# Attention on one Trainium2 core: the product with V in two halves of its columns, the maximum pieces of a step in three parts around them

## The chip, the core and the metric

The kernel runs on one core of a Trainium2 chip. The metric is the device time of one execution in microseconds. Work is spread over the engines of the core: TensorE (PE in the rows, its weight loads PEld), VectorE (DVE), ScalarE (ACT), GpSimd (POOL) and the DMA queues, issued here by SyncE (SP). Each engine runs its own instruction stream in order, and they meet at semaphores.

## The reference, cut to what matters

The program is half a feed-forward block, a two-way Mamba block, and the feed-forward block again. Each feed-forward block begins with causal attention over 4 sequences of 2048 tokens, with 16 heads of 16 that share 4 key and value heads:

```
attn = jnp.einsum('bqhd,bkhd->bhqk', q, k) * scale
attn = jnp.where(causal, attn, jnp.float32(-jnp.inf))
attn = jax.nn.softmax(attn, axis=-1)
out = jnp.einsum('bhqk,bkhd->bqhd', attn, v).reshape(B, S, C)
```

The change is in this attention alone, which is run twice in an execution.

## The kernel before

`attention` makes N = 16 iterations, one for each sequence and key head; an iteration serves the 4 query heads (REP) of that key head. In an iteration there are NB = 40 steps. A step is one block (qb, kb): 512 query tokens (qb of 0 to 3) against 128 key tokens (kb up to the diagonal). On the diagonal only the last 384, 256 or 128 query columns of a block are computed.

For each step s the engines do this:

- TensorE, `score` (L739): the transposed scores of the 4 heads, keys on partitions and queries along the row, one PSUM bank for each head (banks 0 to 3). Two heads lie in different row halves of the array and run beside each other. Heads 0 and 1 wait until ScalarE has read the banks of heads 0 and 1 of the step before, heads 2 and 3 until it has read those of 2 and 3.
- ScalarE (L794): two exponentials of two heads each, PSUM to SBUF tile `e`, with room for 4 steps.
- GpSimd (L641): the causal mask on diagonal blocks of `e`.
- TensorE, `weighted` (L705), for the step LAG = 2 earlier: the product of `e` with V in f32, accumulated in bank 4 over a qb. Each head takes 32 columns of the array, so the four heads run beside each other. In the trace each f32 matmul of the program is two records, so that one product is eight.
- TensorE, `maximum` (L674, and L678 for a diagonal mask): the softmax needs the row maximum of the scores before the exponential, so scores with queries on partitions are computed a second time, ahead of use, in 144 pieces an iteration. A piece is up to 512 columns in one PSUM bank. Pieces come in pairs: even ones lie in the lower row half of the array, odd ones in the upper, and two of a pair run beside each other.
- VectorE, `reduce` (L833): one maximum over each piece.

The pieces, the turned outputs and the turned maxima go round three PSUM banks (5, 6, 7) in the order of use. TensorE waits in `bank_is_free` until the use three places earlier has been read.

`share(s)` says which pieces a step has; `spread` has dealt them out by a cost for each step. Steps 5, 7, 16 and 27 have six pieces, step 2 has none, steps 3, 6, 10, 11, 14, 22, 23, 26, 38 and 39 have two, and the other 25 have four. The last iteration of a call has only the pieces of its steps 0 to 7. In steps 2, 6, 14 and 26 an output is copied to tile `o` by ScalarE (L809) and turned on TensorE (L713); VectorE then normalises it (L851, L854). In steps 8 and 19 the maxima are turned (L692).

The order on TensorE inside a step is written out by hand. Before, it is: four scores, the first part of the pieces (two of four, two of six, none of two), the whole product with V, the rest of the pieces, and then what is turned.

Of the kernel before, what the change touches and what calls it, by code (L numbers as in the profile page):

```python
# [14 lines left out]
CH = 512  # L15
# [15 lines left out]
class Phase:  # L31
# [9 lines left out]
    def sb(self, name, shape, dtype=F32):  # L41
        return self.ctx.enter_context(self.nc.sbuf_tensor(f"{self.tag}_{name}", shape, dtype))

    def sem(self, name):
        self.sems.append(self.nc.alloc_semaphore(f"{self.tag}_{name}"))
        return self.sems[-1]
# [364 lines left out]
VW = 32  # L411
# [3 lines left out]
def attention(nc, tag, psum, ident, unscale, qp, kp, v_in, ao, B, S):  # L415
# [6 lines left out]
    N = B * KVH  # L422
    NBUF = 3
    assert N > 1 and (N - 1) % NBUF == 0
    blocks = [(qb, kb) for qb in range(NQB) for kb in range(TT * (qb + 1))]
    NB = len(blocks)
# [10 lines left out]
    PB = 4  # L437
    LAG = 2
    E0, PV0 = 1, PB - 1

    def diag(s):
        qb, kb = blocks[s]
        return kb - TT * qb

    def closes(s):
        return s >= 0 and blocks[s][1] == TT * (blocks[s][0] + 1) - 1
# [52 lines left out]
    def share(s, last=False):  # L499

        return [("tail", n) for n in tail[s]] if s < D else [] if last else [("head", n) for n in head[s - D]]
# [14 lines left out]
    def out_of(it, qb):  # L516

        return it - 1 if qb == NQB - 1 else it
# [10 lines left out]
    with Phase(nc, tag) as ph:  # L529
# [3 lines left out]
        V = [sb(f"v{p}", [P, S // P, VW]) for p in range(NBUF)]  # L533
        E = sb("e", [P, PB, REP, CH])
# [12 lines left out]
        s_ps, e_ready, masked, pv = sem("s_ps"), sem("e_ready"), sem("masked"), sem("pv")  # L547
        o_sb, oT_ps, recip, normed, stored = sem("o_sb"), sem("oT_ps"), sem("recip"), sem("normed"), sem("stored")
        BANK_O = 4
# [14 lines left out]
        with nc.Block() as block:  # L564
# [81 lines left out]
            def _(pe):  # L646
# [3 lines left out]
                def bank_is_free(when, it, use):  # L650

                    found = used_before(when, it, use)
                    if found is None:
                        pe.wait_ge(m_red, T)
                        return
                    at, (kind, n) = found
                    if kind == "tail":
                        pe.wait_ge(m_red, at * NP + n + 1)
                    elif kind == "head":
                        pe.wait_ge(m_red, (at + 1) * NP + n + 1)  # L660
                    elif kind == "out":
                        pe.wait_ge(normed, out_of(at, n) * NQB + n + 1)
                    elif kind == "max":
                        pe.wait_ge(m_high, 2 * (at + 1 - n) + n + 1)
                        pe.wait_ge(m_low, 2 * (at + 1 - n) + n + 1)
# [16 lines left out]
                def maxima(when, it, par, todo):  # L682

                    for kind, n in todo:
                        if (kind, n) == ("head", 0):
                            pe.wait_ge(loaded[(par + 1) % NBUF], LOADS * ((it + 1) // NBUF + 1))
                        bank_is_free(when, it, (kind, n))
                        maximum(par if kind == "tail" else (par + 1) % NBUF, n, turn_bank(when, (kind, n)))
# [2 lines left out]
                    hold(pe, n_max, 2 * it + g + 1, pe_passed)  # L691
                    nc.tensor.transpose(psum[0:MR, turn, 0:P], nm[:, :, :].rearrange("p h i -> p (h i)"), ident[:, :]).then_inc(mT_ps, 1)  # L692

                def weighted(it, par, s):

                    qb, kb = blocks[s]
                    off = max(diag(s), 0) * P
                    pe.wait_ge(e_ready, E0 + 2 * (it * NB + s + 1))
                    if diag(s) >= 0:
                        n_diag = sum(diag(z) >= 0 for z in range(s + 1))  # L700
                        pe.wait_ge(masked, it * NQB * TT + n_diag)
                    if kb == 0:
                        pe.wait_ge(o_sb, it * NQB + qb)
                    for h in range(REP):
                        ins = nc.tensor.matmul(psum[32 * h:32 * h + VW, BANK_O, off:CH], V[par][:, kb, :],  # L705
                                               E[:, s % PB, h, off:CH], start=kb == 0, stop=closes(s),
                                               tile_position=(0, 32 * h))
                    ins.then_inc(pv, 1)

                def turn_output(it, qb, turn):  # L710
                    pe.wait_ge(o_sb, it * NQB + qb + 1)
# [12 lines left out]
                def step(it, par, when):  # L724
                    q, k = Q[par], K[par]
                    last = (par + 2) % NBUF
                    for s in range(NB):
                        qb, kb = blocks[s]
                        off = max(diag(s), 0) * P
                        if s == 0:  # L730
                            pe.wait_ge(m_in, PUTS * (2 * it + 1))
                        if s == s_half:
                            pe.wait_ge(m_in, PUTS * (2 * it + 2))

                        def score(h):
                            if h % 2 == 0:
                                pe.wait_ge(e_ready, E0 + 2 * (it * NB + s) + h // 2 - 1)
                            at = slice(h % 2 * ROWS, h % 2 * ROWS + SROWS)
                            ins = nc.tensor.matmul(psum[:, h, off:CH], k[at, kb * P:(kb + 1) * P],  # L739
                                                   q[at, qb * CH // (HALF * P), h // 2, qb * CH % (HALF * P) + off:qb * CH % (HALF * P) + CH],  # L740
                                                   start=True, stop=True, tile_position=(h % 2 * ROWS, 0))
                            if h % 2:
                                ins.then_inc(s_ps, 1)

                        todo = share(s, when == "last")
                        half = len(todo) // 4 * 2
                        score(0)
                        score(1)  # L750
                        score(2)
                        score(3)
                        maxima(when, it, par, todo[:half])
                        if s >= LAG:
                            weighted(it, par, s - LAG)
                        elif when != "first":
                            weighted(it - 1, last, NB + s - LAG)
                        maxima(when, it, par, todo[half:])
                        out = back_close(s)
                        if out is not None and not (when == "first" and s <= LAG):  # L760
                            bank_is_free(when, it, ("out", out))
                            turn_output(out_of(it, out), out, turn_bank(when, ("out", out)))
                        if s == TURN1:
                            bank_is_free(when, it, ("max", 1))
                            turn_maxima(it, 1, turn_bank(when, ("max", 1)))
                        if s == TURN0 and when != "last":
                            bank_is_free(when, it, ("max", 0))
                            turn_maxima(it + 1, 0, turn_bank(when, ("max", 0)))
                phase_steps(pe, step)
                for s in range(NB - LAG, NB):  # L770
                    weighted(N - 1, (N - 1) % NBUF, s)
                pe.wait_ge(m_red, N * NP)
                pe.wait_ge(m_low, 2 * N)
                pe.wait_ge(normed, N * NQB - 1)
# [1368 lines left out]
```

## Time and profile before

| What | Value |
|---|---|
| Median of 3 runs | 8606.55 us (8600.69 to 8619.03) |
| The profiled execution: its own time | 8600.78 us |
| The profiled execution: its span | 8599.0 us |
| First attention's iterations, start of scores of the first to that of the last | 272.5 to 1770.1 us |
| Second attention's | 6528.5 to 8033.9 us |
| TensorE busy in the span | 7649.1 us (89%) |
| VectorE busy | 7351.8 us (85%) |
| ScalarE busy | 5097.1 us (59%) |

An engine's busy time counts the spans of its instructions laid over one another. The matmuls are pipelined, and each record reaches some 0.2 us beyond the issue of the next, so that the time a matmul takes of TensorE is read here from the start of one group to the start of the next, not from its duration.

### The profile page before, as it was taken

How to read it: one execution, taken by the hardware profiler on the slowest of the kernel's cores; microseconds unless marked ns; L12 is line 12 of the kernel's file. 1: busy time of each engine (PE TensorE's matmuls, PEld its weight loads, DVE VectorE, ACT ScalarE, POOL GpSimd, SP SyncE). 2: the span in 40 equal slices, each digit the busy share in tenths (PEclk: the TensorE clock that was granted, in tenths of full speed). 3: DMA queues.
4: the chain of work that ended last, by engine and by line, in shares of the span. 5: the costliest groups of instructions: out<-in, count | busy, mean ns of one | idle time of the engine just before them, and what ended most of it. 6: DMA issues, size and time to landing. Idle time of an engine off the chain costs nothing. (4 is left out here: it accounts for less than half of the span.)

```text
span 8599.0 us, 133275 instructions
## 1 busy us (share of the span) xinstructions
PE 7649.1 (89%) x38899; PEld 3079.3 (36%) x38900; DVE 7351.8 (85%) x10758; ACT 5097.1 (59%) x7698; POOL 3712.1 (43%) x1828
## 2 busy tenths in 40 slices
PE   6999999989898888888888888888779999999899
PEld 3333333335543333333333333333443333333355
DVE  6988888958868999999979999999458988988588
ACT  3577777762256666666656555555224777777622
POOL 0010111000018999999969999999300010011000
PEclk8899999989999999999999999999987999999899
DMA  6101111012262222222233333333561011011122
GB/s 174 17 20 19 19 21 25 13 45 75 67 234 85 83 82 83 83 83 82 82 100 101 101 99 101 101 97 100 166 196 29 20 19 20 19 19 19 37 72 65
DMA packets 542812, 617.68 MB, mean 72 GB/s; under 512 B 195969, under 2 KB 353921, under 8 KB 538081
## 3 DMA queue, kind: packets, MB, share of 16 engines
q1 hardware_dynamic: 537568, 576.35, 22.8%
q0 software_dynamic: 4608, 33.56, 1.9%
q8 instruction: 314, 5.14, 0.2%
q14 instruction: 322, 2.63, 0.1%
HBM read 411.41 MB, written 163.76 MB: 67 GB/s over the span
## 5 line engine op out<-in xcount | busy, mean ns | idle before, releaser
L833 DVE TENSOR_REDUCE ffn_att_mx<-psum 128x1 f32<-128x512 f32 (+3 forms) x4608 | 2725.7, 653 | 354.9 <-PE psum L674 199.4
L794 ACT ACTIVATE ffn_att_e<-psum,unscale 128x1024 f32<-128x1024 f32 (+3 forms) x2560 | 2378.7, 985 | 750.0 <-PE psum L739 744.0
L641 POOL TENSOR_SCALAR_AFFINE_SELECT ffn_att_e<-ffn_att_e 128x512 f32<-128x512 f32 x512 | 326.1, 637 | 3007.8 <-ACT ffn_att_e L794 3007.8
L674 PE MATMUL psum<-ffn_att_k,ffn_att_q 48*128 48x512 f16 (+3 forms) x5120 | 1433.5, 366 | 173.5 <-DMA ffn_att_v<-v 58.1
L1697 POOL TENSOR_TENSOR scan_r_h<-scan_r_h,scan_r_cs 128x1024 f32<-128x1024 f32 x512 | 1207.7, 2451 | 148.2 <-ACT scan_r_state L1860 144.7
L1697 POOL TENSOR_TENSOR scan_f_h<-scan_f_h,scan_f_cs 128x1024 f32<-128x1024 f32 x512 | 1204.7, 2446 | 117.0 <-ACT scan_f_state L1860 114.8
L705 PE MATMUL psum<-ffn_att_e,ffn_att_v 128*32 128x512 f32 (+3 forms) x10240 | 1234.2, 555 | 8.0 <-ACT ffn_att_o L809 2.6
L1776 PE MATMUL psum<-scan_f_h,ident 128*128 128x512 f32 x2048 | 1002.5, 630 | 83.9 <-POOL scan_f_h L1697 83.4
L1776 PE MATMUL psum<-scan_r_h,ident 128*128 128x512 f32 x2048 | 980.6, 620 | 75.3 <-POOL scan_r_h L1697 74.5
L1900 ACT ACTIVATE psum<-scan_r_dt,scan_r_an 128x512 f32<-128x512 f32 x1024 | 698.0, 682 | 460.2 <-DVE scan_r_h L1992 460.0
L674 PEld LDWEIGHTS psum<-ffn_att_k,ffn_att_q 48*128 48x128 f16 x5120 | 394.5, 94 | 1554.0 <-DVE ffn_att_mx L833 1268.3
L1900 ACT ACTIVATE psum<-scan_f_dt,scan_f_an 128x512 f32<-128x512 f32 x1024 | 697.5, 681 | 422.6 <-DVE scan_f_h L1992 422.3
L739 PE MATMUL psum<-ffn_att_q,ffn_att_k 50*128 50x512 f16 (+3 forms) x5120 | 809.0, 353 | 62.4 <-issue 27.3
L1992 DVE TENSOR_TENSOR_SCAN scan_r_h<-psum,scan_r_state,scan_r_db 128x512 f32<-128x512 f32 x704 | 845.2, 1261 | 6.1 <-ACT psum L1900 6.0
L1992 DVE TENSOR_TENSOR_SCAN scan_f_h<-psum,scan_f_state,scan_f_db 128x512 f32<-128x512 f32 x704 | 840.8, 1260 | 8.6 <-ACT psum L1900 8.5
L1776 PEld LDWEIGHTS psum<-scan_f_h,ident 128*128 128x128 f32 x2048 | 389.3, 199 | 678.6 <-issue 437.6
L1776 PEld LDWEIGHTS psum<-scan_r_h,ident 128*128 128x128 f32 x2048 | 386.1, 196 | 647.8 <-issue 438.6
L1180 DVE SCALAR_TENSOR_TENSOR ffn_out_acc<-psum,ffn_out_comb,ffn_out_acc 128x256 f32<-128x256 f32 x896 | 433.3, 484 | 64.9 <-PE psum L1045 29.8
L678 PE MATMUL psum<-ffn_att_mask,ffn_att_pick 64*128 64x128 bf16 x4096 | 435.2, 221 | 0.0
L1958 DVE TENSOR_TENSOR scan_r_db<-scan_r_du,psum 128x2048 f32<-128x2048 f32 x177 | 404.8, 2287 | 24.5 <-DVE scan_r_h L1992 3.9
L1958 DVE TENSOR_TENSOR scan_f_db<-scan_f_du,psum 128x2048 f32<-128x2048 f32 x177 | 404.9, 2287 | 23.7 <-PE psum L1751 3.4
L983 POOL TENSOR_TENSOR ffn_out_ul<-ffn_out_uT,ffn_out_uh 128x1024 f16<-128x1024 f32 x32 | 68.1, 2128 | 811.5 <-ACT ffn_out_uh L1094 811.5
(261 smaller groups left out, 9895.2 us busy)
## 6 DMA issues: line engine op xcount, KB each, us to landing
scan_f_cs<-scan_f_bcd SPq DMA_DIRECT2D x264, 256.0 KB, 3.1
scan_r_cs<-scan_r_bcd SPq DMA_DIRECT2D x264, 256.0 KB, 3.2
scan_f_bs<-scan_f_bcd SPq DMA_DIRECT2D x82, 256.0 KB, 3.4
scan_r_bs<-scan_r_bcd SPq DMA_DIRECT2D x82, 256.0 KB, 3.4
scan_f_win<-xp SPq DMA_DIRECT2D x18, 1036.0 KB, 6.7
scan_r_win<-xp SPq DMA_DIRECT2D x18, 1036.0 KB, 7.0
mamba_out_ys<-yz SPq DMA_DIRECT2D x18, 1024.0 KB, 7.3
scan_r_yi<-y SPq DMA_DIRECT2D x17, 1024.0 KB, 9.3
```

The source lines that it names most:

```text
L674: ins = nc.tensor.matmul(psum[:, turn, j * w:(j + 1) * w], q[at, i // HALF, pair, i % HALF * P:(i % HALF + 1) * P], k[at, c * P:c * P + w] ...
L678: ins = nc.tensor.matmul(psum[:, turn, (j + 1) * w - P:(j + 1) * w], pick[rows_at, 1 - hh + z, :], mask[rows_at, 1 - hh + z, :], start=Fal ...
L705: ins = nc.tensor.matmul(psum[32 * h:32 * h + VW, BANK_O, off:CH], V[par][:, kb, :], E[:, s % PB, h, off:CH], start=kb == 0, stop=closes(s ...
L739: ins = nc.tensor.matmul(psum[:, h, off:CH], k[at, kb * P:(kb + 1) * P], q[at, qb * CH // (HALF * P), h // 2, qb * CH % (HALF * P) + off:q ...
L794: nc.scalar.activation(E[:, s % PB, 2 * hp:2 * hp + 2, off:CH], psum[:, 2 * hp:2 * hp + 2, off:CH], ACT.Exp, scale=unscale[:, 0:1]).then_i ...
L833: nc.vector.reduce_max(mx[:, hh * 2 + pairs[0]:hh * 2 + pairs[1], i // HALF, i % HALF, c // TT], psum[:, turn, 0:(pairs[1] - pairs[0]) * w ...
L1180: nc.vector.scalar_tensor_tensor(acc[:, e % 2, :], psum[:, BANKS_E[(n // 2) % 4], (e % 2) * C:(e % 2 + 1) * C], comb[par][:, t, e:e + 1], ...
L1697: nc.gpsimd.tensor_tensor(hh, hh, cs[:, n % NCS, :].unsqueeze(1).to_broadcast([P, 2, CH]), ALU.mult).then_inc(hc_ready, 1)
L1776: ins = nc.tensor.matmul(psum[:, m, :], ident[:, :], h[n % NH][:, m, :], start=False, stop=n == DS - 1)
L1900: nc.scalar.activation(psum[:, BANK_A + k % 2, :], dt[par][:, m, :], ACT.Exp, scale=an[:, m, n:n + 1]).then_inc(decay, 1)
L1958: nc.vector.tensor_tensor(db[b_turn(par, n)][:, :, :], du[par][:, :, :], psum[:, BANK_B, :].unsqueeze(1).to_broadcast([P, DM, CH]), ALU.mu ...
L1992: nc.vector.tensor_tensor_scan(h[n % NH][:, m, flip], psum[:, BANK_A + k % 2, flip], made_b[:, m, flip], state[:, n, m:m + 1], ALU.mult, A ...
```

## The change

The product with V is issued in two halves of its columns (`part` 0 and 1, the middle being halfway between `off` and 512). The pieces of the step are cut in three: a first third, the first half of the product, a second third, the second half, and the last third. With four pieces the parts are 1, 1, 2, with two pieces 0, 1, 1, and with six 2, 2, 2. The sum of pieces of each step, their order, and all other engines' instructions stay as they were. Semaphore `pv` is raised at the second half alone, as the wait on `e` stands ahead of both halves.

```diff
-                def weighted(it, par, s):
+                def weighted(it, par, s, part):
...
                     off = max(diag(s), 0) * P
+                    mid = (off + CH) // 2
+                    lo, hi = (off, mid) if part == 0 else (mid, CH)
                     pe.wait_ge(e_ready, E0 + 2 * (it * NB + s + 1))
...
                     for h in range(REP):
-                        ins = nc.tensor.matmul(psum[32 * h:32 * h + VW, BANK_O, off:CH], V[par][:, kb, :],
-                                               E[:, s % PB, h, off:CH], start=kb == 0, stop=closes(s),
+                        ins = nc.tensor.matmul(psum[32 * h:32 * h + VW, BANK_O, lo:hi], V[par][:, kb, :],
+                                               E[:, s % PB, h, lo:hi], start=kb == 0 and part == 0, stop=closes(s) and part == 1,
                                                tile_position=(0, 32 * h))
-                    ins.then_inc(pv, 1)
+                    if part == 1:
+                        ins.then_inc(pv, 1)
...
                         todo = share(s, when == "last")
-                        half = len(todo) // 4 * 2
+                        cuts = [len(todo) * k // 3 for k in range(4)]
                         score(0)
                         score(1)
                         score(2)
                         score(3)
-                        maxima(when, it, par, todo[:half])
-                        if s >= LAG:
-                            weighted(it, par, s - LAG)
-                        elif when != "first":
-                            weighted(it - 1, last, NB + s - LAG)
-                        maxima(when, it, par, todo[half:])
+                        for part in range(2):
+                            maxima(when, it, par, todo[cuts[part]:cuts[part + 1]])
+                            if s >= LAG:
+                                weighted(it, par, s - LAG, part)
+                            elif when != "first":
+                                weighted(it - 1, last, NB + s - LAG, part)
+                        maxima(when, it, par, todo[cuts[2]:])
```

On TensorE, in steps 22 and 23 and the start of 24, the program before has these rows. The names are: `ffn_att_q,ffn_att_k` with `ffn_att_k` last are scores of a step, `ffn_att_k,ffn_att_q` a maximum piece, `ffn_att_e,ffn_att_v` the product with V of one head.

```order
L739 MATMUL psum<-ffn_att_q,ffn_att_k 128x256 x4
L705 MATMUL psum<-ffn_att_e,ffn_att_v 32x512 x4
L674 MATMUL psum<-ffn_att_k,ffn_att_q 128x512 x2
L739 MATMUL psum<-ffn_att_q,ffn_att_k 128x128 x4
L705 MATMUL psum<-ffn_att_e,ffn_att_v 32x384 x4
L674 MATMUL psum<-ffn_att_k,ffn_att_q 128x512 x2
L739 MATMUL psum<-ffn_att_q,ffn_att_k 128x512 x4
```

The same two steps of the changed program, on the same engine:

```order
L742 MATMUL psum<-ffn_att_q,ffn_att_k 128x256 x4
L707 MATMUL psum<-ffn_att_e,ffn_att_v 32x256 x4
L674 MATMUL psum<-ffn_att_k,ffn_att_q 128x512
L707 MATMUL psum<-ffn_att_e,ffn_att_v 32x256 x4
L674 MATMUL psum<-ffn_att_k,ffn_att_q 128x512
L742 MATMUL psum<-ffn_att_q,ffn_att_k 128x128 x4
L707 MATMUL psum<-ffn_att_e,ffn_att_v 32x192 x4
L674 MATMUL psum<-ffn_att_k,ffn_att_q 128x512
L707 MATMUL psum<-ffn_att_e,ffn_att_v 32x192 x4
L674 MATMUL psum<-ffn_att_k,ffn_att_q 128x512
L742 MATMUL psum<-ffn_att_q,ffn_att_k 128x512 x4
```

The pair of pieces, which stood together behind the product, is now one piece between its halves and one behind them.

The second place is step 28 with the scores of step 29, where a step has four unmasked pieces of 512 columns; TensorE before:

```order
L739 MATMUL psum<-ffn_att_q,ffn_att_k 128x512 x4
L674 MATMUL psum<-ffn_att_k,ffn_att_q 128x512 x2
L705 MATMUL psum<-ffn_att_e,ffn_att_v 32x512 x4
L674 MATMUL psum<-ffn_att_k,ffn_att_q 128x512 x2
L739 MATMUL psum<-ffn_att_q,ffn_att_k 128x512 x4
```

And in the changed program, at the same place:

```order
L742 MATMUL psum<-ffn_att_q,ffn_att_k 128x512 x4
L674 MATMUL psum<-ffn_att_k,ffn_att_q 128x512
L707 MATMUL psum<-ffn_att_e,ffn_att_v 32x256 x4
L674 MATMUL psum<-ffn_att_k,ffn_att_q 128x512
L707 MATMUL psum<-ffn_att_e,ffn_att_v 32x256 x4
L674 MATMUL psum<-ffn_att_k,ffn_att_q 128x512 x2
L742 MATMUL psum<-ffn_att_q,ffn_att_k 128x512 x4
```

Of the first pair one piece now stands ahead of the product and one between its halves; the second pair stays together behind it.

## Rows read from the trace of the kernel before

**Rows 1.** The page's busy time of each engine, of the whole span.

```profile
PE 7649.1 (89%) x38899; PEld 3079.3 (36%) x38900; DVE 7351.8 (85%) x10758; ACT 5097.1 (59%) x7698; POOL 3712.1 (43%) x1828
```

**Rows 2.** Windows, one iteration each: start:end, length, busy by engine, clock, DMA share, GB/s.

```profile
472.26:571.12 98.86, 94.10 (x789) 32.12 (x786) 88.09 (x157) 76.61 (x86) 10.19 (x16) 0.98 0.11 20
...
1077.71:1175.40 97.69, 92.86 (x789) 31.83 (x787) 88.09 (x157) 76.60 (x86) 10.20 (x16) 1.00 0.10 21
```

**Rows 3.** Windows, steps 10 to 11, 14 to 20, 26 to 37, 38 to 39.

```profile
1103.39:1106.38 2.99, 2.99 (x42) 0.99 (x38) 2.16 (x4) 2.11 (x4) 0.83 (x3) 1.00 0.02 3
...
1110.74:1130.70 19.96, 18.87 (x145) 6.21 (x145) 18.01 (x33) 15.80 (x17) 0.00 (x0) 1.00 0.04 8
...
1140.74:1172.41 31.67, 30.29 (x231) 8.96 (x233) 29.62 (x51) 25.90 (x26) 1.13 (x2) 1.00 0.03 5
1172.41:1175.40 2.99, 2.99 (x38) 1.00 (x34) 2.36 (x4) 2.10 (x4) 0.78 (x2) 1.00 0.00 0
```

**Rows 4.** Waits, iteration at 1077.71 us: total us, times, longest.

```profile
PEld psum L674 <- DVE ffn_att_mx L833: 39.8, 76, 0.8
...
DVE ffn_att_mx L833 <- PE psum L674: 4.7, 8, 1.0
```

**Rows 5.** Timeline of TensorE, two steps of four pieces: start us, us, group.

```profile
454.43 0.90 PE L674 MATMUL psum<-ffn_att_k,ffn_att_q 48*128 48x512 f16 x2
455.25 1.07 PE L705 MATMUL psum<-ffn_att_e,ffn_att_v 128*32 128x512 f32 x8
456.25 0.39 PE L674 MATMUL psum<-ffn_att_k,ffn_att_q 48*128 48x512 f16 x2
456.48 0.60 PE L739 MATMUL psum<-ffn_att_q,ffn_att_k 50*128 50x512 f16 x4
456.91 0.90 PE L674 MATMUL psum<-ffn_att_k,ffn_att_q 48*128 48x512 f16 x2
```

**Rows 6.** Timeline, TensorE alone at 457.45 us: the second piece of the last group.

```profile
457.43 0.39 PE L674 MATMUL psum<-ffn_att_k,ffn_att_q 48*128 48x512 f16 x1
```

**Rows 7.** Timeline of VectorE in the same steps, one reduction a row.

```profile
455.39 0.68 DVE L833 TENSOR_REDUCE ffn_att_mx<-psum 128x1 f32<-128x512 f32 x1
...
455.99 0.68 DVE L833 TENSOR_REDUCE ffn_att_mx<-psum 128x1 f32<-128x512 f32 x1
...
456.68 0.69 DVE L833 TENSOR_REDUCE ffn_att_mx<-psum 128x1 f32<-128x512 f32 x1
```

**Rows 8.** Timeline of ScalarE in the same steps, with the idle time before.

```profile
456.90 2.12 ACT L794 ACTIVATE ffn_att_e<-psum,unscale 128x1024 f32<-128x1024 f32 x2 [0.37 <-PE psum L739]
```

**Rows 9.** Timeline of TensorE in steps 10, 11 and the start of 12, 13.

```profile
1103.39 0.39 PE L739 MATMUL psum<-ffn_att_q,ffn_att_k 50*128 50x256 f16 x4
1103.71 1.06 PE L705 MATMUL psum<-ffn_att_e,ffn_att_v 128*32 128x512 f32 x8
1104.70 0.40 PE L674 MATMUL psum<-ffn_att_k,ffn_att_q 48*128 48x512 f16 x2
1104.93 0.28 PE L678 MATMUL psum<-ffn_att_mask,ffn_att_pick 64*128 64x128 bf16 x4
1105.05 0.28 PE L739 MATMUL psum<-ffn_att_q,ffn_att_k 50*128 50x128 f16 x4
1105.26 0.85 PE L705 MATMUL psum<-ffn_att_e,ffn_att_v 128*32 128x384 f32 x8
1106.04 0.40 PE L674 MATMUL psum<-ffn_att_k,ffn_att_q 48*128 48x512 f16 x2
...
1107.64 0.64 PE L705 MATMUL psum<-ffn_att_e,ffn_att_v 128*32 128x256 f32 x8
1108.22 0.69 PE L674 MATMUL psum<-ffn_att_k,ffn_att_q 48*128 48x512 f16 x2
```

**Rows 10.** Windows, step 6 in two iterations; the clock is the third number from the end.

```profile
485.66:489.77 4.11, 4.11 (x19) 1.25 (x18) 2.59 (x5) 2.12 (x2) 0.00 (x0) 0.58 0.65 145
688.36:690.94 2.58, 2.58 (x20) 0.91 (x21) 2.14 (x4) 2.02 (x2) 0.00 (x0) 1.00 0.98 191
```

More of the change, by code:

```diff
@@ L770, in _ @@
                 for s in range(NB - LAG, NB):
-                    weighted(N - 1, (N - 1) % NBUF, s)
+                    weighted(N - 1, (N - 1) % NBUF, s, 0)
+                    weighted(N - 1, (N - 1) % NBUF, s, 1)
                 pe.wait_ge(m_red, N * NP)
```

## The prediction, made before the changed kernel was run

> **What bounds the kernel now.** The page's busy times [rows 1] say only that TensorE and VectorE are both near full. The change touches the attention, so I cut one iteration out by windows: from the first scores to those of the next iteration it lasts 97.69 us at full clock, 98.86 us where the clock is 0.98 [rows 2]. VectorE is busy for 88.1 of it, TensorE for 92.9, ScalarE for 76.6: no engine is idle enough to be left out, and which one sets the pace must be read from each kind of step.
>
> *Steps of four pieces (25 of 40).* The scores of this step are issued at 456.48 us and the first piece at 456.91 (0.43 for the scores), the pair behind the product at 456.25, 0.23 ahead of them; the product takes 1.00, from 455.25 to 456.25 [rows 5]. The step's period is 2.48 (454.43 to 456.91). The two pieces ahead of the product are not issued together: the second comes at 457.43, 0.52 behind the first [rows 6], as its bank is still being reduced; such waits for VectorE are 39.8 us of an iteration at the weight loads [rows 4] (much of this lies under a running product). On VectorE one reduction starts 0.60 after the other if its piece is there (455.39, 455.99), and once a step 0.69 after it (456.68) [rows 7]. So VectorE needs 4 x 0.60 = 2.40 of 2.48: it is the bound, and the largest gain to be had in such a step is 0.08. ScalarE is busy for 2.12 and idle for 0.37 [rows 8].
>
> *Steps of two pieces (10).* Steps 10 and 11 last 2.99 together and TensorE is busy in all of it, VectorE for 2.16; steps 38 and 39 read alike [rows 3]. There TensorE's own stream is the bound: scores, product, pair, with no wait in it [rows 9].
>
> Where VectorE is idle in an iteration, 4.7 us and more of it are waits for pieces [rows 4], mostly behind these light steps.
>
> **The change part by part.** It adds no work to VectorE, ScalarE, GpSimd or a queue. On TensorE it does three things.
>
> (a) A product in halves. From product to the next group a 512-column product takes 1.00 [rows 5], one of 384 columns 0.78 (1105.26 to 1106.04), one of 256 columns 0.58 (1107.64 to 1108.22) [rows 9]. That is 0.21 for each 128 columns and some 0.14 that does not depend on the columns. Two halves of 256 take 1.14 to 1.16 by the rounding of the starts; I take 1.14: **+0.14**; two of 192 (0.47 each, an estimate on the same line) +0.16.
>
> (b) A switch from a piece into a product. The four scores of 256 columns need 0.22 (half of 0.43), but the product follows 0.32 behind them [rows 9], so entering a product costs 0.10. A lone piece at 512 columns is a stream of 0.21 (its 0.22 as half the scores), and with the switch 0.32.
>
> (c) A broken pair. A pair leaves 0.23 behind it [rows 5]; two lone pieces take 0.21 each. A masked pair takes 0.35 (1104.70 to 1105.05 [rows 9]), so that a mask adds 0.12 for the pair, and adds it twice if the pair is broken.
>
> For a step of two: before 0.10 + 1.00 + 0.23 behind the scores, after 0.10 + 0.57 + 0.32 + 0.57 + 0.23: **+0.46**, and +0.58 if masked. For a step of four, before 0.33 + 1.00 + 0.23 = 1.56, after 0.32 + 0.57 + 0.32 + 0.57 + 0.23 = 2.01: **+0.45**, so that TensorE's stream grows from 1.99 to 2.44 with the scores. For a step of six (pairs stay whole) +0.24; for step 2 some +0.04.
>
> Below nothing these costs cannot go: no matmul is taken away. Their upper end is that a half costs as much as the nearest whole in the rows, 0.58 and not 0.57, and that each lone piece with its mask waits for its bank as well.
>
> Three lots of steps answer differently.
>
> *Light steps bound by TensorE.* All of it shows: steps 10 and 11 +0.58 and +0.57 (masked), 22 and 23 +0.46 and +0.45, 39 +0.45, 3 (384 columns, masked) +0.50, 38 +0.28, since its 1.72 now holds a wait for VectorE that its stream of 1.54 does not need. Step 6 +0.45. Sum **+3.7**. Nothing covers them: ScalarE and VectorE have less to do in these steps than 1.5 us.
>
> *Steps of four at 512 columns.* The period becomes the larger of TensorE's 2.44 and VectorE's 2.40, where it was 2.48. Scores 2 and 3 wait for ScalarE, whose 2.12 for a step begin 0.42 behind the scores (456.48, 456.90) [rows 5, 8], which leaves 2.45. So unmasked steps gain 0.03 to 0.04. Masked ones (18, 30) had 2.71 and get 2.44 + 3 x 0.12 = 2.80, so lose 0.08; steps 15 and 34, with a masked pair broken first, lose 0.05. Steps 14 to 20 now take 19.96 and steps 26 to 37 31.67, with VectorE busy 18.0 and 29.6 [rows 3]. Adding the new streams, with six-piece steps at VectorE's pace, I get about 19.8 and 31.4: **-0.4** together.
>
> *The rest* (0 to 2, 4, 5, 7 to 9, 12, 13, 21, 24, 25) has small products (64 or 128 columns a half) or slack: +0.13 at step 4, some 0.1 at others, together **+0.2**.
>
> An iteration gets +3.5 us. Two calls have 15 iterations each with all pieces (the last has few pieces and stays with ScalarE): 30 x 3.5 = 105 us. Against it stands the clock: step 6 takes 4.11 at a granted clock of 0.58 in one iteration and 2.58 at full clock in another [rows 10]; about half of the iterations have such a drop, behind steps in which TensorE did little. A denser TensorE may lose some: 8 us off. That gives 8600.8 + 97 = 8698 for the profiled kind of run, whose time stands 5.8 below the median of the runs shown; for the median 8606.6 + 97, I say **8700**.
>
> **A rule weighed against the rows.** The row says that a halved product costs 0.14 more. The Trainium skill (TensorE: Matmul & The Clock Gate, Back-to-back issue gap) gives the isolated spacing of matmuls as columns over 2.4 GHz plus 2.5 ns, by which a halving would cost some 5 ns. The same page (Part 3, The mechanism) lets a weight load overlap matmuls in flight only where the row group differs, by which product and piece, which share rows, can't hide each other's load; the trace agrees with the latter, with the 0.10 at the entry and the 0.14 at the exit.
>
> **The rivals.**
>
> 1. *As worked out: TensorE's stream is what the light steps wait for, +3.5 an iteration.* Own range +1.4 to +6.3 an iteration (steps of four gain the whole 0.08 each at one end, at the other they keep half of the waits that the trace now shows over the larger of the streams, some 6 of 98), 8640 to 8790. Chance 0.62.
>
> 2. *The switches are hidden.* If the weights of the next group come in while the last one streams, (a) and the second 0.10 fall away and a step of two pays only for the broken pair, 0.22. For: the program allows loads ahead. Against: the row of 256 columns pays the whole 0.14 where a pair follows. Seven light steps then cost 1.6 and twenty steps of four gain 0.08 each, 1.6: no change, 8606. Chance 0.08.
>
> 3. *Faster: VectorE is kept fed and TensorE's slack absorbs everything.* TensorE's streams alone, summed over the 40 steps by the costs above, go from 75 to 93 us, under 97.7. If the three banks let a TensorE-bound step lend time to its VectorE-bound neighbour, the iteration goes to some 95: 30 x -2.5, 8530. It decides if, behind a light step, the reductions still queued cover the longer stream, so that VectorE is never idle there. For: a piece between the halves arrives 0.5 earlier than before in terms of TensorE work. Against: three banks hold 1.8 us of reductions, and VectorE is idle already in the light steps. Chance 0.15.
>
> 4. *Much slower: two engines at the same pace.* A step of four has 2.44 on TensorE, 2.40 on VectorE and 2.45 through ScalarE. Any wait for one now delays the others, where 0.5 of TensorE slack took it up. If the surplus over the larger stream, about 6 us an iteration today, stays as it is on top of a sum of 100, an iteration takes 106: +8.4, 8850. Against: in steady steps every bank comes free 0.1 or more ahead of its use. Chance 0.15.
>
> **How the numbers follow.** The time is that of rival 1. Differences within 0.2% (17 us) can't be told from none. Slower: 0.62 + 0.15, plus a little of 2: 0.78. Faster 0.15, same 0.07. The range goes from 8590, which takes in rival 2, to 8800, which takes in all of 1 and the near end of 4; outside are most of 3 and part of 4, about 0.2.
>
> **What would show it.** In the changed profile: the product's group of 256 columns followed 0.57 later by the piece (right for a); a lone piece followed 0.32 later by the product (b, c); steps 10 to 11 at 4.1 us and 38 to 39 at 3.7, all busy on TensorE; steps of four at 2.44 to 2.46; the waits of L674's weights for VectorE well below 39.8 an iteration. Wrong would be: steps of two that did not grow (rival 2), steps 14 to 20 or 26 to 37 shorter by over 1 us (rival 3), or longer by over 1 (rival 4).

## The result, and the profile after

The changed kernel takes 8711.53 us (median of 4 runs, 8708.62 to 8716.01), the kernel before, beside it, 8605.13 us (4 runs, 8600.69 to 8619.03). The ratio is 1.0122, with an interval of 1.011 to 1.0134: slower by 1.2%. The forecast was 8700 in a range of 8590 to 8800.

The page after, with its span and the busy time of each engine:

```profile
span 8712.4 us, 154363 instructions
...
PE 7853.2 (90%) x49139; PEld 3311.1 (38%) x49140; DVE 7408.8 (85%) x10758; ACT 5091.6 (58%) x7698; POOL 3710.0 (43%) x1828
```

Against [rows 1] TensorE has 10,240 more matmuls and is busy 204 us longer, and the span grew by 113.4 (8712.4 - 8599.0). VectorE has the same instructions.

Windows of the kernel after, columns as in [rows 2]: one whole iteration at full clock, steps 10 to 11, 14 to 20, 26 to 37, and 38 to 39.

```profile
1427.94:1528.20 100.26, 97.55 (x1112) 38.44 (x1108) 89.72 (x157) 76.42 (x86) 10.15 (x17) 1.00 0.10 21
1453.74:1457.54 3.80, 3.80 (x56) 1.49 (x51) 2.77 (x5) 2.10 (x4) 1.18 (x3) 1.00 0.01 2
1462.29:1482.74 20.45, 19.86 (x202) 7.35 (x199) 18.29 (x33) 15.46 (x17) 0.00 (x0) 1.00 0.04 9
1493.24:1524.56 31.32, 31.19 (x328) 10.96 (x329) 29.49 (x51) 25.86 (x26) 0.98 (x2) 1.00 0.03 6
1524.56:1528.20 3.64, 3.64 (x54) 1.32 (x48) 3.15 (x6) 2.10 (x4) 1.13 (x3) 1.00 0.00 0
```

The iteration went from 97.69 [rows 2] to 100.26: +2.57, and TensorE is now busy for all but 2.7 us of it. Against [rows 3] steps 10 to 11 lost 0.81, steps 38 to 39 0.65, steps 14 to 20 0.49, and steps 26 to 37, of which ten have four pieces, gained 0.35.

The waits of the same iteration, columns as in [rows 4]:

```profile
PEld psum L674 <- DVE ffn_att_mx L838: 19.6, 51, 0.6
...
DVE ffn_att_mx L838 <- PE psum L678: 4.4, 15, 0.5
DVE ffn_att_mx L838 <- PE psum L674: 3.8, 16, 0.5
```

The second and third of these rows are VectorE's waits for pieces. In the kernel before they were the 4.7 us of [rows 4] and this row of the same view:

```profile
DVE ffn_att_mx L833 <- PE psum L678: 3.3, 7, 0.8
```

The pieces' wait for VectorE fell from 39.8 [rows 4] to 19.6: TensorE has used up half of its slack. That wait was slack and not the pace, so its fall bought nothing by itself. VectorE's own waits for pieces, which rival 3 would have shortened, stayed the same in sum: 8.0 us before, 8.2 after.

TensorE in a step of four pieces, kernel after (start us, us, group), and VectorE there:

```profile
1512.03 0.60 PE L742 MATMUL psum<-ffn_att_q,ffn_att_k 50*128 50x512 f16 x4
1512.47 0.38 PE L674 MATMUL psum<-ffn_att_k,ffn_att_q 48*128 48x512 f16 x1
1512.77 0.64 PE L707 MATMUL psum<-ffn_att_e,ffn_att_v 128*32 128x256 f32 x8
1513.35 0.39 PE L674 MATMUL psum<-ffn_att_k,ffn_att_q 48*128 48x512 f16 x1
1513.66 0.64 PE L707 MATMUL psum<-ffn_att_e,ffn_att_v 128*32 128x256 f32 x8
1514.23 0.39 PE L674 MATMUL psum<-ffn_att_k,ffn_att_q 48*128 48x512 f16 x2
1514.46 0.38 PE L742 MATMUL psum<-ffn_att_q,ffn_att_k 50*128 50x512 f16 x2
...
1511.61 3.74 DVE L838 TENSOR_REDUCE ffn_att_mx<-psum 128x1 f32<-128x512 f32 x6
```

From scores to scores it is 2.43 (1512.03 to 1514.46), where [rows 5] had 2.48. A half product is followed 0.58 and 0.57 later (1513.35, 1514.23), a lone piece ahead of a product 0.30 and 0.31 later. VectorE does six reductions without a gap. Both engines are full, as the terms of the prediction had it; which of the two sets the 2.43 these rows don't tell.

TensorE in steps 22 and 23, two pieces each, kernel after:

```profile
1485.33 0.38 PE L742 MATMUL psum<-ffn_att_q,ffn_att_k 50*128 50x256 f16 x4
1485.64 0.64 PE L707 MATMUL psum<-ffn_att_e,ffn_att_v 128*32 128x256 f32 x8
1486.21 0.39 PE L674 MATMUL psum<-ffn_att_k,ffn_att_q 48*128 48x512 f16 x1
1486.53 0.64 PE L707 MATMUL psum<-ffn_att_e,ffn_att_v 128*32 128x256 f32 x8
1487.10 0.39 PE L674 MATMUL psum<-ffn_att_k,ffn_att_q 48*128 48x512 f16 x1
1487.10 0.49 PE L742 MATMUL psum<-ffn_att_q,ffn_att_k 50*128 50x128 f16 x4
1487.53 0.53 PE L707 MATMUL psum<-ffn_att_e,ffn_att_v 128*32 128x192 f32 x8
```

0.57 for a half and 0.32 for the piece between the halves are there again. But the last piece of step 22 and the first score of step 23 start together, at 1487.10. Alone, the last piece occupies one row half of the array, and a score that lies in the other half runs beside it. The pair it replaces filled both halves and held the scores up for 0.23 (1485.10 to 1485.33 in this trace too). So step 22 takes 1.77, 0.23 more than its 1.54 before, where I had forecast 0.46 more. The Trainium skill (TensorE: Matmul & The Clock Gate, Part 3, The mechanism) says that a weight load overlaps matmuls in flight only where the row group differs; these two equal starts agree with it.

Part of the piece is paid for one product later, though. The scores of step 23 have only 128 columns, and the piece that runs beside them has 512. The product follows the start of these scores by 0.43 (1487.10 to 1487.53); in the kernel before, at the same place, by 0.26:

```profile
1134.85 0.33 PE L739 MATMUL psum<-ffn_att_q,ffn_att_k 50*128 50x128 f16 x4
1135.11 0.85 PE L705 MATMUL psum<-ffn_att_e,ffn_att_v 128*32 128x384 f32 x8
```

So 0.17 of the lone piece sticks out behind the short scores. In step 24, whose scores have 512 columns, nothing does: the lone piece of step 23 starts with them (1488.78) and the next piece follows 0.44 later (1489.22), where four such scores alone took 0.43 [rows 5].

**Where the 113.4 us are.** The undisturbed iteration gives 30 x 2.57 = 77. The 30 iterations in sum went from 3003.0 to 3124.3, by 121.3, so 44 lie in iterations that something disturbs. The last iterations of the two calls became 3.8 shorter, and all that lies outside the iterations about 4 shorter. What disturbs is for the most part TensorE's clock. (The other disturbance is that TensorE stops for some 3 to 4 us at the end of step 39, at full clock, in the same six iterations of both kernels; it cost 22 us in sum before and 18 after. Steps 4 to 9 carry the difference: over their undisturbed length they cost 24 us in sum before and 75 after.) Windows of steps 6 and 7, kernel before, one iteration with a fall of the clock and one without:

```profile
485.66:492.90 7.24, 6.96 (x43) 2.23 (x44) 5.55 (x11) 4.24 (x4) 0.00 (x0) 0.76 0.78 119
1091.06:1097.18 6.12, 5.80 (x44) 1.96 (x44) 5.56 (x11) 4.24 (x4) 0.00 (x0) 1.00 0.78 125
```

The same steps, kernel after:

```profile
494.17:504.34 10.17, 10.17 (x61) 2.89 (x63) 6.30 (x11) 4.34 (x5) 0.00 (x0) 0.50 0.44 85
1441.69:1447.67 5.98, 5.98 (x60) 2.33 (x61) 5.64 (x11) 4.33 (x5) 0.00 (x0) 1.00 0.55 110
```

At full clock these two steps are even 0.14 shorter than before. But where the clock falls, both run wholly at 0.50, the lower of its levels (1.2 GHz), and cost 4.2 us more, where the fall before cost 1.1; most falls of the two kernels are near these two. Summed over steps 4 to 9 of the 30 iterations, low clock lasted 68 us before (in 17 iterations) and 190 after (in 18): as often, but three times as long.

### The profile page after: what moved, and what is told of

It reads as the page before. It is cut to its first block and busy times, and to the rows that moved or that the text cites. A ratio compares the mean times of both kernels' runs of the same rounds, so it can differ in the third digit from the quotient of the medians.

```text
span 8712.4 us, 154363 instructions
## 1 busy us (share of the span) xinstructions
PE 7853.2 (90%) x49139; PEld 3311.1 (38%) x49140; DVE 7408.8 (85%) x10758; ACT 5091.6 (58%) x7698; POOL 3710.0 (43%) x1828
## 5 line engine op out<-in xcount | busy, mean ns | idle before, releaser
L838 DVE TENSOR_REDUCE ffn_att_mx<-psum 128x1 f32<-128x512 f32 (+3 forms) x4608 | 2775.9, 656 | 399.0 <-PE psum L678 185.2
L674 PE MATMUL psum<-ffn_att_k,ffn_att_q 48*128 48x512 f16 (+3 forms) x5120 | 1518.2, 371 | 76.0 <-DMA ffn_att_v<-v 56.8
L707 PE MATMUL psum<-ffn_att_e,ffn_att_v 128*32 128x256 f32 (+3 forms) x20480 | 1500.1, 369 | 13.9 <-ACT ffn_att_o L814 9.2
L742 PE MATMUL psum<-ffn_att_q,ffn_att_k 50*128 50x512 f16 (+3 forms) x5120 | 838.4, 358 | 71.7 <-ACT ffn_att_e L799 53.5
L674 PEld LDWEIGHTS psum<-ffn_att_k,ffn_att_q 48*128 48x128 f16 x5120 | 412.4, 94 | 1114.4 <-DVE ffn_att_mx L838 684.8
L707 PEld LDWEIGHTS psum<-ffn_att_e,ffn_att_v 128*32 128x32 f32 x20480 | 421.7, 109 | 606.4 <-issue 359.7
L678 PE MATMUL psum<-ffn_att_mask,ffn_att_pick 64*128 64x128 bf16 x4096 | 466.8, 223 | 0.0
```

The costliest lines, as they stand in the source:

```text
L674: ins = nc.tensor.matmul(psum[:, turn, j * w:(j + 1) * w], q[at, i // HALF, pair, i % HALF * P:(i % HALF + 1) * P], k[at, c * P:c * P + w] ...
L678: ins = nc.tensor.matmul(psum[:, turn, (j + 1) * w - P:(j + 1) * w], pick[rows_at, 1 - hh + z, :], mask[rows_at, 1 - hh + z, :], start=Fal ...
L707: ins = nc.tensor.matmul(psum[32 * h:32 * h + VW, BANK_O, lo:hi], V[par][:, kb, :], E[:, s % PB, h, lo:hi], start=kb == 0 and part == 0, s ...
L838: nc.vector.reduce_max(mx[:, hh * 2 + pairs[0]:hh * 2 + pairs[1], i // HALF, i % HALF, c // TT], psum[:, turn, 0:(pairs[1] - pairs[0]) * w ...
```

## The experiments

**Two theories.** *A*, mine: the light steps, whose pace is TensorE's stream, pay for the switches between kinds of matmul, and the steps of four pay nothing. *B*, its rival, was that one part alone costs all of it: the halving of a product as such, or the broken pairs as such. From the fourth run on a further question was what lengthens the low clock. All kernels but the last two move only the three numbers of this shortened code, with `a, b, whole = half, 0, True` for the order before and `third, two_thirds, False` for the changed one:

```diff
+    maxima(todo[:a])
+    weighted(...)             # whole, or its first half
+    maxima(todo[a:b])         # nothing where whole
+    weighted(...)             # second half, where not whole
+    maxima(todo[b:])          # todo[a:] where whole
```

"Undisturbed" is the shortest kind of iteration, at full clock and without the stop at its end, to be held against 97.69 before and 100.26 after. Ratios are to the kernel before, run beside it.

**1. The halves back to back, pieces as before.**

```diff
-    a, b, whole = third, two_thirds, False
+    a, b, whole = half, half, False
```

> The product is issued in two halves, but back to back; the pieces stand as before the change (two or none ahead, the rest behind). All of the reference is computed. Theory A (the cost lies in the second switch between product and piece and in the broken pairs, not in halving as such): inside a product the second of the two passes already begins without a gap, so a half costs at most 0.03 us more, 40 steps x 0.03 = 1 us an iteration where TensorE is the bound, less elsewhere: +0.3 to +1.2 us an undisturbed iteration (97.69 before, 100.25 after the change), 8610 to 8640 us. Theory B (each half has a fixed cost of its own of 0.14 us, or the doubled count of matmuls costs): most of the slowdown stays, +1.5 us or more an iteration, over 8660 us.

8600.67 us, ratio 0.9992 (0.9982 to 1.0001), undisturbed 97.86. TensorE at one product of this kernel:

```profile
1644.52 1.07 PE L707 MATMUL psum<-ffn_att_e,ffn_att_v 128*32 128x256 f32 x16 [0.19 <-ACT ffn_att_o L817]
1645.52 0.39 PE L674 MATMUL psum<-ffn_att_k,ffn_att_q 48*128 48x512 f16 x2
```

Sixteen records of 256 columns take 1.00, as eight of 512 do in [rows 5]. Halving is free, and the time came out even below the 8610 to 8640 of my theory; the undisturbed iteration is 0.17 longer, far from the 2.57 of the change. The 0.14 of term (a) is paid for leaving a product towards another kind of matmul, and is paid twice only where something stands between the halves.

**2. Halves, but pairs unbroken** (0, 2, 2 of four pieces; 0, 0, 2 of two; 2, 2, 2 of six).

```diff
-    a, b, whole = third, two_thirds, False
+    a, b, whole = 2 * (third // 2 if len(todo) == 6 else 0), 2 * (len(todo) // 2 * 2 // 3), False
```

> Two halves with pieces between them, but pairs are never broken: steps of four have 0, 2, 2 pieces, steps of two 0, 0, 2, steps of six 2, 2, 2. All of the reference is computed. Theory A: in steps of two only the halving without a switch is left (0.03), in steps of four TensorE's stream is 0.43 + 0.10 + 0.57 + 0.33 + 0.57 + 0.23 = 2.23, under VectorE's 2.40, so an undisturbed iteration is 97.3 to 98.5, and the time 8600 to 8640 us. Theory B (the halving and the count of matmuls cost): over 8660 us. If feeding VectorE between the halves is worth anything, it shows here as steps of four under 2.48.

8608.02, ratio 1.0003 (0.9993 to 1.0012), undisturbed 97.39. In a step of four the pair now stands between the halves, and an iteration is 0.3 shorter, but low clock in steps 4 to 9 rose to 130 us and took the 9 us back. In 10 of its iterations steps 6 and 7 together last over 8 us, though step 6 has the order of before with the product in two adjacent halves.

**3. Whole product, pairs broken around it.**

```diff
-    a, b, whole = third, two_thirds, False
+    a, b, whole = (1 if len(todo) in (2, 4) else half), 0, True
```

> The product stays whole; in steps of two and four one piece goes ahead of it and the rest behind, so that the first pair is broken by it. All of the reference is computed. Theory A: a step of two has 0.32 + 1.00 + 0.23 = 1.55 behind its scores against 1.33 before, +0.22, masked +0.34; over the ten light steps about +1.8 us an iteration, steps of four stay at VectorE's pace (2.40 to 2.48): 99.0 to 99.8 an undisturbed iteration, 8640 to 8670 us. Theory B (broken pairs cost nothing, since two pieces never ran beside each other in effect): no more than 98.0 an iteration, under 8620 us.

8615.4, ratio 1.0013 (1.0003 to 1.0023), undisturbed 97.24. Here my expectation failed: over an iteration, broken pairs around a whole product cost nothing, and what the time has over that of before is not in the undisturbed iteration. TensorE, this kernel:

```profile
1644.47 0.39 PE L674 MATMUL psum<-ffn_att_k,ffn_att_q 48*128 48x512 f16 x1
1644.47 0.60 PE L742 MATMUL psum<-ffn_att_q,ffn_att_k 50*128 50x512 f16 x3
1644.92 0.38 PE L674 MATMUL psum<-ffn_att_k,ffn_att_q 48*128 48x512 f16 x1
1644.92 0.37 PE L742 MATMUL psum<-ffn_att_q,ffn_att_k 50*128 50x512 f16 x1
1645.22 0.64 PE L707 MATMUL psum<-ffn_att_e,ffn_att_v 128*32 128x256 f32 x8
```

The last piece of one step starts with the scores of the next (1644.47), and the next step's first piece with its last score (1644.92). Both lone pieces lie beside scores. From 1644.47 to the product it is 0.75, and four scores with an unbroken pair take as much by the rows of before, 0.43 + 0.33. In the change it is the piece between two halves that has no such neighbour.

**4 and 5. The change only in steps 8 to 39, and only in steps 0 to 7.**

```diff
-    a, b, whole = third, two_thirds, False
+    a, b, whole = (third, two_thirds, False) if s >= 8 else (half, 0, True)
```

> The changed order in steps 8 to 39, the order of before in steps 0 to 7. All of the reference is computed. In the changed kernel the granted clock is low for some 10 us in steps 6 and 7 of about half of the iterations, at 4.1 us each, where before it was low for 3 us at 1.5 us each; some 40 of the 113 us of slowdown. Theory A (what TensorE does in steps 0 to 7 alone decides on that drop): the drop in steps 6 and 7 costs 1.5 us again, an undisturbed iteration is +1.8 to +2.4, 8660 to 8680 us. Theory B (the drop comes of the whole iteration's density or of anything else in the program): drops of 4 us stay, 8695 to 8715 us.

8667.2, ratio 1.0078 (1.0062 to 1.0095), undisturbed 99.96; a fall of the clock in step 6 costs 1.1 to 1.6, as in the kernel before.

The fifth is the same with `s < 8`.

> The complement of the run before: the changed order in steps 0 to 7, the order of before in steps 8 to 39. All of the reference is computed. Theory A (TensorE's work in steps 0 to 7 decides on the drop of the clock there): the drops of some 4 us in steps 6 and 7 are back in about half of the iterations, and an undisturbed iteration is only 0.2 to 0.6 us over 97.69; together 8640 to 8665 us. Theory B (drops depend on the whole iteration): no long drops, 8610 to 8625 us.

8644.86 (7 runs, 8623.63 to 8669.09), ratio 1.0049 (1.0034 to 1.0064), undisturbed 97.90; its falls in steps 6 and 7 cost 2.7 to 4.3 us. So steps 8 to 39 carry 2.27 of the 2.57 an iteration, and steps 0 to 7 the long falls. The two losses, 0.78% and 0.49%, add up to 1.27%, against 1.22% for the whole.

**6 and 7. The change only in the ten steps of two pieces, and only in the others.**

```diff
-    a, b, whole = third, two_thirds, False
+    a, b, whole = (third, two_thirds, False) if len(todo) == 2 else (half, 0, True)
```

> The changed order in the ten steps with two pieces alone (3, 6, 10, 11, 14, 22, 23, 26, 38, 39). All of the reference is computed. Theory A (the light steps are TensorE's, so its longer stream shows in full): in the changed kernel these ten are 3.3 us longer than before, so an undisturbed iteration is 100.2 to 101.0, and 8675 to 8720 us. Theory B (what is lost there comes back in the heavy steps behind them, whose VectorE has less of a queue): +1.5 us or less an iteration, under 8655 us.

8746.73, ratio 1.0167 (1.015 to 1.0184), slower than the whole change and than the 8720 of my theory. Window of one undisturbed iteration, this kernel:

```profile
795.54:895.51 99.97, 94.24 (x871) 33.39 (x868) 89.47 (x157) 76.11 (x86) 10.14 (x17) 1.00 0.09 20
```

The light steps alone give +2.28. The rest of the loss is the clock: 258 us of low clock in steps 4 to 9, in 24 of 30 iterations.

The seventh has `len(todo) != 2`.

> The changed order in the steps with four or six pieces alone. All of the reference is computed. Theory A: an undisturbed iteration loses the light steps' 3.3 us from 100.25 and so is 96.8 to 97.4, 0.3 to 0.9 under before; whether it shows in the time hangs on the clock drops in steps 5 to 8, which keep the changed order but for step 6: 8580 to 8640 us. Theory B (broken pairs and switches in the heavy steps are half of the slowdown): 98.5 us or more an iteration, 8640 us or more.

8607.4, ratio 1.0001 (0.9992 to 1.0011), undisturbed 97.86. I had expected 0.3 to 0.9 less and got +0.17: for the heavy steps the change is a wash. 2.28 + 0.17 = 2.45 of the 2.57.

**8. In steps of two, the pair ahead of the whole product.**

```diff
-    a, b, whole = third, two_thirds, False
+    a, b, whole = min(len(todo), 2), 0, True
```

> The product is whole and pairs are whole; only in the ten steps with two pieces the pair goes ahead of the product, where before it went behind. All of the reference is computed. TensorE's stream is the same length (0.33 + 1.00 + 0.12 before the next scores against 0.10 + 1.00 + 0.23). Theory A (VectorE idles in and behind the light steps for want of pieces, some 8 us an iteration): the pieces come 1.1 us earlier, an undisturbed iteration is 96.0 to 97.4, 8560 to 8600 us. Theory B (only TensorE's stream counts in the light steps): no change, 8600 to 8612 us.

8609.7, ratio 1.0004 (0.9995 to 1.0014), undisturbed 97.41. My theory failed: an iteration gains only 0.28, and the low clock in steps 4 to 9 rose from 68 to 126 us and ate it. The time is what the rival said.

**9 and 10. Step 6 alone.** First the change without it, then nothing but it:

```diff
-    a, b, whole = third, two_thirds, False
+    a, b, whole = (third, two_thirds, False) if s != 6 else (half, 0, True)
```

> The changed kernel with the order of before in step 6 alone. All of the reference is computed. In the changed kernel steps 6 and 7 take 5.98 us at full clock and 10.17 us where the clock falls, before 6.12 and 7.24. Theory A (the split product with its two lone pieces in step 6 is what keeps the clock low): the drop costs 1 to 1.5 us again, some 35 to 45 us off 8711: 8660 to 8680 us. Theory B (any of the longer streams from step 0 on does it, or the pieces of step 7): drops of 4 us stay, 8695 to 8712 us.

8686.76, ratio 1.009 (1.0074 to 1.0105), undisturbed 100.36. Windows of its steps 6 and 7, with and without a fall:

```profile
488.42:496.07 7.65, 7.61 (x51) 2.36 (x53) 5.51 (x11) 4.34 (x5) 0.00 (x0) 0.78 0.54 99
801.08:807.17 6.09, 6.05 (x52) 2.27 (x52) 5.53 (x11) 4.34 (x5) 0.00 (x0) 1.00 0.62 114
```

The fall costs 1.6 here, not 4.2. The time fell by 25 us and not by the 35 to 45 expected, as some iterations had more low clock elsewhere, in steps 0 to 3.

> The kernel of before with the changed order in step 6 alone, of 40. All of the reference is computed. At full clock steps 6 and 7 together are 0.1 us shorter in the changed kernel, so the stream predicts no change at all. Theory A (step 6's order makes the drop of the clock long): 8625 to 8650 us from this one step. Theory B: 8600 to 8612 us.

8653.2, ratio 1.0047 (1.0031 to 1.0062), a little over the 8625 to 8650 expected of this one step. Windows of this kernel: an undisturbed iteration, then steps 6 to 8 with a fall and without.

```profile
1396.11:1493.83 97.72, 92.90 (x796) 31.97 (x794) 88.21 (x157) 76.53 (x86) 10.18 (x16) 1.00 0.10 21
1197.21:1212.21 15.00, 14.86 (x91) 5.41 (x92) 8.80 (x17) 6.35 (x6) 0.64 (x1) 0.54 0.30 56
1409.46:1419.11 9.65, 9.23 (x90) 3.93 (x90) 8.59 (x17) 6.36 (x6) 0.55 (x1) 1.00 0.47 90
```

The undisturbed iteration is that of before (97.72 against 97.69), and yet the kernel is 0.5% slower: one step's order, in 195 us of low clock over 19 iterations. Together the two runs show that step 6's order is enough for long falls, and that it is not the only place where they come about.

**11. Take the fall away instead.** The fall comes behind step 5, in which TensorE waits for VectorE with six pieces, while step 6 has two. This kernel has the order before everywhere, and one pair moved from step 5 to step 6:

```diff
+    tail[5], tail[6] = tail[5][:-2], tail[5][-2:] + tail[6]
```

> The order of before inside every step, but one pair of pieces is moved from step 5 (six to four) to step 6 (two to four). All of the reference is computed. Step 5 is VectorE's for 3.42 us, of which TensorE streams some 1.6, and the clock falls right behind it in 17 of 30 iterations. Theory A (TensorE's waiting in step 5 is what the drop follows, and VectorE's six reductions there are 0.4 us longer than the even deal needs): an undisturbed iteration is 0.1 to 0.5 us shorter and most drops in step 6 are gone, 8560 to 8592 us. Theory B (the drop comes of the turn and the short products of steps 1 to 4, and the deal is a wash): 8598 to 8612 us.

8551.09 (5 runs, 8545.45 to 8557.61), ratio 0.9931 (0.9917 to 0.9944), 9 us faster than the best I expected. Windows of one iteration and of its steps 5 to 6, this kernel, and those steps in the kernel before:

```profile
1362.66:1459.91 97.25, 92.70 (x788) 31.75 (x786) 88.11 (x157) 76.42 (x86) 10.18 (x16) 1.00 0.11 21
1372.58:1378.30 5.72, 5.16 (x39) 1.66 (x36) 5.68 (x11) 5.06 (x6) 0.00 (x0) 1.00 0.70 173
```

```profile
1087.63:1093.63 6.00, 5.21 (x39) 1.70 (x36) 5.53 (x10) 5.08 (x6) 0.00 (x0) 1.00 0.58 165
```

No iteration of the 30 has a fall in steps 4 to 9, where 17 had one before. VectorE's 5.68 of 5.72 shows that a step of six and one of two became two of four with VectorE hardly ever idle. TensorE's idle time in the two steps fell only from 0.79 (6.00 - 5.21) to 0.56 (5.72 - 5.16). Of the gain, 30 x 0.44 = 13 us are the undisturbed iteration, and 24 us are the falls of steps 4 to 9 that are gone. Whether it is the fewer pieces in step 5 or the more work in step 6 that keeps the clock up was not separated.

**12. The same for the other neighbours.** Kernel 11, and pairs moved from step 15 to 14, from 16 to 15 and from 27 to 26:

```diff
+    for to, at in ((14, 15), (15, 16), (26, 27)):
+        head[to - D], head[at - D] = head[to - D] + head[at - D][:2], head[at - D][2:]
```

> The order of before inside every step and the even deal of the run before (a pair from step 5 to step 6), and three more pairs moved one step forward in the same way: from 15 to 14, from 16 to 15, from 27 to 26. All of the reference is computed. Theory A (VectorE's six reductions in a step are a queue that TensorE must wait for, and a light step ahead of it has room): an undisturbed iteration is 0.3 to 1.0 us under 97.25, 8520 to 8545 us. Theory B (steps 14 and 26 hold an output that is turned, which needs a bank and 0.7 us of VectorE, so that the moved pairs only wait earlier): 8545 to 8570 us.

8525.01 (5 runs, 8515.2 to 8532.65), ratio 0.9914 (0.9901 to 0.9928). Windows of one iteration, of steps 14 to 16 and of 26 to 27; then those steps in the kernel before:

```profile
1351.12:1447.21 96.09, 92.19 (x789) 31.44 (x786) 88.05 (x157) 76.50 (x86) 10.20 (x16) 1.00 0.10 21
1383.71:1392.15 8.44, 8.35 (x73) 3.14 (x73) 7.86 (x15) 7.28 (x8) 0.00 (x0) 1.00 0.08 16
1413.04:1418.90 5.86, 5.72 (x45) 2.03 (x47) 5.66 (x11) 4.95 (x6) 0.00 (x0) 1.00 0.00 0
```

```profile
1110.74:1119.82 9.08, 8.56 (x71) 3.17 (x70) 7.74 (x15) 7.28 (x8) 0.00 (x0) 1.00 0.07 14
1140.74:1147.07 6.33, 5.94 (x44) 1.92 (x45) 5.37 (x11) 5.13 (x6) 0.00 (x0) 1.00 0.10 21
```

The five steps gain 0.64 + 0.47 = 1.11, and the iteration 1.16 over kernel 11. Four iterations have a fall in steps 4 to 9 again, 9 us of low clock in sum. Dealing the pieces evenly over neighbours beats both kernels, by 0.9% and by 2.1% (8525.01 against 8711.53, not measured side by side), without touching the order inside a step.

## Why the prediction was right, point by point

Sign, place and mechanism are those of its first rival: the light steps wait for TensorE's stream, and experiments 6 and 7 show that they carry the loss. The total, 8700 against 8711.5, is closer than its terms, since two errors cancel; that is luck.

- **Term (a), +0.14 for a product in halves: right in size, wrong in cause.** 0.57 behind each half; but the cost is the way out of a product into a piece, and back-to-back halves cost nothing (experiment 1).
- **Term (b), 0.32 for a lone piece ahead of a product: right**, 0.30 to 0.32 after.
- **Term (c), a broken pair, the last piece of a step included: the mis-sized one.** "After 0.10 + 0.57 + 0.32 + 0.57 + 0.23" counts 0.23 for the last piece of a step of two. It runs beside the next scores and measured nothing where these have 512 columns, and 0.17 where they have 128 (steps 22 to 23). Steps 22 and 23 lost 0.65 and not 0.91, steps 10 and 11 0.81 and not 1.15 (masked, "4.1 us" forecast, 3.80 measured), steps 38 and 39 0.65 and not 0.73, and step 3, by the medians, 0.24 and not 0.50. With step 6 (+0.45, as forecast) the light steps give +2.8 instead of +3.7.
- **Step 6's +0.45 did not stay.** By the medians step 7 fell from 3.55 to 2.95, so that the two together are 0.14 shorter. A six-piece step behind a light one takes up what that one lost, and so did step 27 (-0.52) behind step 26 (+0.43); it was to be seen as the slack of step 7, which I had put with "the rest".
- **Steps of four.** Forecast 2.44 to 2.46, measured 2.43. Steps 26 to 37 came down by 0.35, where 0.3 was forecast. Steps 14 to 20 went up by 0.49, where -0.2 was forecast; by the medians step 15 lost 0.27 and step 18, masked, 0.12. Experiment 7 gives +0.17 for the change in the heavy steps alone, not a gain either.
- **The rest.** Forecast +0.2. The sum of the parts above (2.80 + 0.49 - 0.35) leaves -0.4 for it. In it steps 2 and 13 went up by 0.28 and 0.50, which I had not seen; step 7's 0.60 and 0.22 less in step 0 pay for both.
- **The clock, -8: wrong in sign.** Windows give +44. I argued that a denser TensorE loses fewer falls. Their number stayed (17 and 18) and each became longer. With +77 for the undisturbed part instead of +105, the errors of -28 and +52 cancel but for 24, of which the last iterations and the rest give back 8: the span grew by 113.4, and +97 was forecast.
- **The rivals.** Hidden switches (2): excluded by the 0.57 and 0.32. VectorE kept fed (3): steps 26 to 37 gained 0.35 of the 1 us it needed, and VectorE's waits for pieces stayed at 8 us an iteration. Two engines at one pace (4): an iteration would have been 106; 100.26 says that two engines filled at 2.43 and 2.40 didn't get in each other's way.

**What stays open.** That the order of step 6 makes the low clock last longer is shown by experiments 9 and 10; that other steps can do it too, by experiment 2, whose step 6 has the order of before, the halves adjacent. Why an order does so is not shown: at full clock TensorE is as busy there as before or more. Nor is it shown why the light steps alone (experiment 6) have more low clock than the whole change. Why an even deal ends the falls is argued from the waits of step 5 and not shown. Splitting steps 13 and 18 from the others was not tried.

## What to carry to other kernels

Count what stands next to an instruction, not the instruction alone: a small matmul that uses half of the array's rows is free beside others that use the other half, as far as they last as long as it does, and costs its stream and a switch on both sides between two that use all rows. A wait that TensorE spends on the bound engine is slack, and filling it with finer pieces pays nothing, while every step that TensorE bounds pays for the switches. Look instead at uneven work between neighbouring steps: evening it out made the iteration 1.6% shorter, and here the falls of the clock in those steps went with it.

## What the runs showed of the hardware that I had not expected

- Halving f32 products is free if the halves are adjacent: 16 records of 256 columns in 1.00 us, as 8 of 512. Leaving for f16 matmuls on 48 rows costs 0.14 (0.57 for a half, where two adjacent ones take 1.00), coming back 0.10 (0.32 from a piece that streams for 0.21).
- A lone piece on one row half and scores on the other have the same start to 0.01 us (1487.10, 1644.47). Behind scores of 128 columns 0.17 of a piece of 512 sticks out.
- A fall of the clock to 0.50 cost 1.1 us over two steps before and 4.2 after, with TensorE busy in all of the 10.17 us. Changing the order of one step in 40 cost 0.5% of the time in that way; moving one pair of pieces out of step 5 took all 17 falls in steps 4 to 9 away and brought 0.7%.
